# Layer-0 cross attention of a two-layer transformer rewritten in the form of the kernel's self attention

## The chip, the cores and the metric

The kernel runs on one core of one Trainium2 chip. The metric is the device time of one execution in microseconds (us). The core has five engines that run their own instruction streams and wait for each other on semaphores: PE (TensorE, matrix products; its weight loads are listed apart as PEld), DVE (VectorE), ACT (ScalarE), POOL (GpSimd) and SP (SyncE, which here only issues DMAs).

## The reference, cut to what matters

Two layers follow each other over x of shape 2 x 1024 x 256. The change lies in the first block of layer 0, in its second attention, which reads a context of 77 rows:

```
x = layernorm(sa + input_tensor, g1, be1)            # sa: causal self attention, 16 heads of 16
q = einsum('bsd,hde->bhse', x, Wq2)                  # 2 x 16 x 1024 x 16
k = einsum('btd,hde->bhte', encoder_output, Wk2)     # 2 x 16 x 77 x 16
v = einsum('btd,hde->bhte', encoder_output, Wv2) + bv2
p = softmax(einsum('bhse,bhte->bhst', q, k) / 4)
ca = einsum('bhst,bhte->bhse', p, v)                 # heads concatenated
x = layernorm(x + ca, g2, be2)
ffn = relu(x @ Wf1 + bf1) @ Wf2 + bf2
x = layernorm(x + ffn, g3, be3)
```

Everything else of the two layers (self attention before it, the feed-forward nets, layer 1's masked cross attention, its second self attention and its mixture of experts) is as it was.

## The kernel before, in words

The 2048 rows of x are 16 tiles of 128. The program is five written-out instruction streams, one for each engine. PSUM has 8 banks of 512 values; `claim` waits until a bank's last reader is done, `filled` and `arrived` pass a filled bank to its reader, `released` and `drained` tell that the reader is done. Each engine works in the order in which its stream is written.

**Self attention of layer 0** runs in 8 groups of 4 heads. A plan (`attention_plan`) is walked by all engines; its iteration n computes the row maxima of group n (operation "max": PE products, DVE reductions) and, interleaved, the scores, exponentials and value products of group n-1 ("score", "pv"). Operands are packed as bf16 parts in 96 rows; the negated maxima are three more rows (99), so that the exponential is taken straight from PSUM. One step has four scores of up to 512 columns, which pass through two banks (4 and 5) to ACT (L1027), and the value product of the step before (four products of 17 columns each, listed as 128*17), which the plan puts behind the step's third score. A unit of the plan is one score; an iteration has 48 units in 12 steps. Iteration 8 has scores only. Each iteration has one ACT copy of 128x1024 (L1042, "evac") right after its second score, so the starts of these copies mark the iterations. Layernorm "g1" of the four row chunks ("norm", lines 1233 to 1251 and 1350 on DVE) and transposes of the normed rows ("turn") lie in iterations 5 to 7 for chunks 0 and 1.

**Cross attention of layer 0** (`cross(0)`) starts when self attention is done. It runs over 32 units: 16 tiles by 2 halves of 8 heads. A unit is: two float32 products of 128x308 (queries against a block-diagonal key matrix KBD), a maximum over each head's 77 scores on DVE (L1532), the subtraction (L1533), the exponential on ACT (L1074), five transposes of the probabilities (L684), their copies on ACT (L1088), five float32 products with the block-diagonal values (128x136), and for each tile a division and an addition to H on DVE (L1539 to L1544). Query projections, the g1 norms and the turning of chunks 2 and 3, the g2 norms and a small low-rank product lie between the units. Then the first feed-forward product (PE, TRR and WF1P) waits for POOL, which takes the power for the last g2 norm and makes the lower parts of the inputs (L1753). POOL also splits the weights WF1 into two parts behind the second g2 norm (L1726, L1727).

Of the kernel before, what the change touches and what calls it, by code (L numbers as in the profile page):

```python
# [20 lines left out]
P = 128  # L21
# [44 lines left out]


# [21 lines left out]
def attention_plan():  # L89


    for n in range(GROUPS + 1):
# [6 lines left out]
        for u in range(units):  # L99
# [10 lines left out]
            if u == 20 and n in (6, 7):  # L110
                yield "turn", n - 6
            if n == 0:
# [18 lines left out]
    yield "out", GROUPS - 1  # L131


def build(nc, a, out):

    ctx = ExitStack()
    with ctx:
# [31 lines left out]
        def w6(n):  # L169
# [47 lines left out]

        QT = region(0, 4096, "p (g s) -> p g s", g=2)
# [5 lines left out]
        CREP = [[v.rearrange("p (k h t) -> p k h t", k=KC, h=HH) for v in pair]  # L224
                for pair in ((region(27904, 1232), W6[:, 0:1232]), (region(23504, 1232), region(24736, 1232)))]
# [51 lines left out]
        scratch = nc.dram_tensor("qk_parts", [B, 2, D, 3, S], BF16, kind="Internal").ap()  # L277

# [20 lines left out]
        sa_used = sem("sa_used")  # L299
        kv_ready = sem("kv_ready")  # L300
# [87 lines left out]
        def _(pe):  # L388
# [66 lines left out]
            def context(layer, wk):  # L455

                loaded(pe, wk[1])
                loaded(pe, "ctx")
                for g in range(2):
                    claim(("kx", layer, g), [4 + g])  # L460
                    for k in range(KC):
                        ins = mm(PS[:, 4 + g, 0:B * T], wk[0][:, k, P * g:P * g + P], ctxT[:, k, :], start=k == 0, stop=k == KC - 1)
                    filled(ins, ("kx", layer, g))

            def queries(layer, wq, c):

                loaded(pe, wq[1])
                for g in range(2):
                    key = ("q", layer, c, g)
                    claim(key, [4 + g])  # L470
                    for k in range(KC):
                        ins = mm(PS[:, 4 + g, :], wq[0][:, k, P * g:P * g + P],
                                 TR[:, k, 512 * c:512 * c + 512], start=k == 0, stop=k == KC - 1)
                    filled(ins, key)
# [39 lines left out]


# [11 lines left out]
            for op, n, *at in attention_plan():  # L527
# [56 lines left out]
                elif op == "turn":  # L584
# [9 lines left out]
                    filled(ins, ("turn", n))  # L594
                elif op == "out":
                    if n == GROUPS - 1:

                        context(0, (w6(4), "wk2"))
                        queries(0, (w6(3), "wq2"), 0)
# [8 lines left out]
            def low_rank(u):  # L608


# [9 lines left out]
                elif u == 20:  # L620
                    drained(pe, "l2")
                    claim("l3", [bank])
                    for k in range(KC):
                        ins = mm(PS[:, bank, D * k:D * k + D], LD2[:, P * k:P * k + P], UPT)
# [1299 lines left out]
```

## Time and profile before

| | |
|---|---|
| median of 3 runs | 1409.89 us (1409.19 to 1413.25) |
| profiled execution, first to last instruction (span) | 1407.6 us |
| time of the profiled execution itself | not listed apart; its span is 2.3 us under the median of the runs |
| PE busy | 1205.0 us, 86% of the span |
| PE weight loads busy | 882.2 us, 63% |
| DVE busy | 909.1 us, 65% |
| ACT busy | 531.9 us, 38% |
| POOL busy | 313.2 us, 22% |
| mean granted TensorE clock | 0.928 |

A busy share is a mean over stages with different limits. The stage that the change rewrites lies between the last value product of self attention and the first product of the feed-forward net. A matmul's busy time holds its latency, so a high share does not tell that PE works at its peak.

### The profile page before, as it was taken

To read this page: it belongs to the slowest core of one execution; us is meant where nothing else is said; L and a number is where in the kernel's file an instruction comes from. 1 tells how busy PE (TensorE), PEld (TensorE's weight loads), DVE (VectorE), ACT (ScalarE), POOL (GpSimd) and SP (SyncE) were. 2 spreads that over 40 slices of the span, in tenths; PEclk is the share of its full clock that TensorE was granted. 3 is DMA by queue.
4 is the path that set the end of the run, shared out by engine and by line. 5 is a ranking of instruction groups with operands and counts; after the bars stand their busy time and mean duration, and the time that the engine had idled before them with its cause. 6 is when DMAs were issued, how large, how long until landed. Compare 5 with 4: busy or idle time off the path is not lost. (4 is left out here: it accounts for less than half of the span.)

```text
span 1407.6 us, 19711 instructions
## 1 busy us (share of the span) xinstructions
PE 1205.0 (86%) x7056; PEld 882.2 (63%) x7056; DVE 909.1 (65%) x1890; ACT 531.9 (38%) x1149; POOL 313.2 (22%) x491
## 2 busy tenths in 40 slices
PE   5779999797888997978859787799999888899999
PEld 2343333233336775866647666699997667789988
DVE  7487666666516887467766888775653445865555
ACT  1325655555652443524413444201003332543333
POOL 5012222222230021534423655100001011500000
PEclk9798999998988999989987988799999999999999
DMA  4850333330000101000003000000002000000000
GB/s 166 179 136 2 46 47 47 46 47 1 2 1 1 65 1 42 1 0 1 1 1 120 1 1 1 1 0 1 1 18 102 1 0 0 1 1 15 16 16 16
DMA packets 25201, 40.35 MB, mean 29 GB/s; under 512 B 5755, under 2 KB 17041, under 8 KB 24465
## 3 DMA queue, kind: packets, MB, share of 16 engines
q1 hardware_dynamic: 25104, 39.09, 11.7%
q8 instruction: 58, 0.95, 0.3%
q14 instruction: 39, 0.31, 0.1%
HBM read 30.49 MB, written 8.39 MB: 28 GB/s over the span
## 5 line engine op out<-in xcount | busy, mean ns | idle before, releaser
L390 PE MATMUL PS<-ARENA 128*17 128x512 f32 (+14 forms) x2528 | 474.0, 400 | 96.5 <-ACT ARENA L1088 21.2
L390 PEld LDWEIGHTS PS<-ARENA 128*128 128x128 f32 (+4 forms) x2528 | 225.7, 141 | 278.2 <-issue 124.6
L1363 DVE TENSOR_REDUCE ARENA<-PS 128x1 f32<-128x128 f32 (+7 forms) x256 | 180.8, 751 | 77.5 <-PE PS L390 76.4
L1027 ACT ACTIVATE ARENA<-PS 128x512 f32<-128x512 f32 (+3 forms) x384 | 173.6, 490 | 147.1 <-PE PS L390 143.5
L390 PE MATMUL PS<-WQKVP,TRR 128*128 128x384 f32 x512 | 132.1, 339 | 3.1 <-DVE ARENA L1613 2.0
L1773 POOL TENSOR_SCALAR_AFFINE_SELECT ARENA<-ARENA 128x128 f32<-128x128 f32 x256 | 73.6, 292 | 224.6 <-ACT ARENA L1027 221.8
L1745 POOL TENSOR_TENSOR rstd<-var,halves 128x4 f32<-128x4 f32 x36 | 37.9, 1051 | 306.0 <-DVE var L1238 305.8
L390 PEld LDWEIGHTS PS<-W2P,INT 128*128 128x128 f32 x768 | 94.9, 188 | 2.8
L390 PE MATMUL PS<-W2P,INT 128*128 128x256 f32 x768 | 95.6, 280 | 0.0
L390 PEld LDWEIGHTS PS<-WQKVP,TRR 128*128 128x128 f32 x512 | 91.4, 188 | 4.6 <-DVE ARENA L1613 2.6
L390 PE MATMUL PS<-TRR,W1P 128*128 128x512 f32 x256 | 88.6, 408 | 5.8 <-ACT BC L973 5.8
L1615 DVE SCALAR_TENSOR_TENSOR ARENA<-PS,rw,ARENA 128x384 f32<-128x384 f32 x112 | 69.2, 618 | 37.4 <-PE PS L390 36.3
L1673 DVE TENSOR_TENSOR INT<-W,INT 128x512 fp32r<-128x512 f32 x64 | 46.2, 729 | 71.2 <-ACT INT L1196 71.0
L390 PE MATMUL PS<-WQKVP,TRL 128*128 128x384 f32 x256 | 86.1, 336 | 0.0
L390 PE MATMUL PS<-ARENA,TR 128*128 128x256 f32 x320 | 81.3, 412 | 2.8 <-ACT TR L957 1.5
L1074 ACT ACTIVATE ARENA<-ARENA 128x616 f32<-128x616 f32 x64 | 46.0, 718 | 98.7 <-POOL ARENA L1842 64.2
L390 PE MATMUL PS<-TR,W 128*128 128x512 f32 x128 | 68.9, 686 | 8.0 <-DVE ARENA L1270 4.8
L390 PEld LDWEIGHTS PS<-ARENA,TR 128*128 128x128 f32 x320 | 65.5, 210 | 13.5 <-issue 2.6
L1195 ACT ACTIVATE W<-PS 128x512 f32<-128x512 f32 x64 | 38.3, 598 | 93.5 <-issue 82.0
L407 PE MATMUL PS<-ident,H 128*128 128x128 f32 x128 | 30.9, 373 | 41.5 <-DVE H L1228 37.5
L1088 ACT COPY ARENA<-PS 128x512 f32<-128x512 f32 (+1 forms) x128 | 47.7, 424 | 42.5 <-PE PS L684 42.2
L390 PE MATMUL PS<-maskq,identb 128*128 128x128 bf16 x272 | 62.6, 231 | 0.0
(198 smaller groups left out, 1909.4 us busy)
## 6 DMA issues: line engine op xcount, KB each, us to landing
ARENA<-qk_parts SPq DMA_DIRECT2D x96, 128.0 KB, 5.8
qk_parts<-ARENA SPq DMA_DIRECT2D x8, 768.0 KB, 3.3
ARENA<-in_w SPq DMA_DIRECT2D x2, 2048.0 KB, 10.5
ARENA<-in_wqkv SPq DMA_DIRECT2D x1, 3072.0 KB, 10.0
X<-in_x SPq DMA_DIRECT2D x4, 512.0 KB, 8.2
ARENA<-in_wf SPq DMA_DIRECT2D x2, 1024.0 KB, 5.5
out_x<-X SPq DMA_DIRECT2D x8, 256.0 KB, 2.2
BC<-in_bcast SPq DMA_DIRECT2D x1, 1920.0 KB, 12.9
```

What stands on the lines that cost most here:

```text
L390: return nc.tensor.matmul(o, lhsT, rhs, start=start, stop=stop, **kw)
L407: ins = nc.tensor.transpose(PS[:, bank, P * k:P * k + P], src[:, i, P * k:P * k + P], ident[:, :])
L1027: ins = nc.scalar.activation(PROB[GRP * (step % 2) + j][:, 0:w], PS[:, uses[key][0], 0:w], ACT.Exp, scale=HD ** -0.5)
L1074: nc.scalar.activation(EX[u % 4], EX[u % 4], ACT.Exp, scale=HD ** -0.5).then_inc(ex_ready, 1)
L1088: released(nc.scalar.copy(PTS[(u - 1) % 4][0:rows, 4 * m:4 * m + cols, :], PS[0:rows, 4 + m, 0:P * cols].rearrange("p (j s) -> p j s", s=P ...
L1195: nc.scalar.activation(INTF[(2 * n + ic) % 4], src, ACT.Gelu)
L1363: ins = v.tensor_reduce(negm[:, n % 2, TPB * j + st:TPB * j + st + 1], PS[:, bank:bank + 2, :].rearrange("p b s -> p (b s)")[:, 0:P * (st ...
L1615: ins = v.scalar_tensor_tensor(out=QKV[:, i, :], in0=src, scalar=w, in1=QKV[:, i, :], op0=ALU.mult, op1=ALU.add)
L1673: v.tensor_tensor(INT[n % 4][:, 1, ic, :], INTF[(2 * n + ic) % 4], INT[n % 4][:, 0, ic, :].bitcast(F32), ALU.subtract).then_inc(int_ready, 1)
L1745: g.tensor_tensor(rstd[:, 4 * k:4 * k + 4], var[:, 4 * k:4 * k + 4], halves[:, 0:4], ALU.pow).then_inc(rstd_ready, 1)
L1773: g.affine_select(out=prob, in_=prob, compare_op=ALU.is_ge, fill=0.0, base=0, pattern=[[1, P]], channel_multiplier=-1).then_inc(cleared, 1)
```

## The change

Layer 0's cross attention no longer calls `cross`; it becomes operations of the plan.

- **Context, once** ("ctxk", "ctxv", in iteration 1): keys are projected and split into three bf16 parts (ACT, DVE, ACT, DVE), written to memory, and read back as XKEYS, 96 rows for each head, plus three rows of ones (12 DMAs of 16x16x77). Values go to XV with a column of ones.
- **Queries, for each chunk of 512 rows** ("xq", "xqm"): projection in float32 as before, but the result is split into three bf16 parts, written to memory (2 DMAs) and read back into the packed form XPACK (12 DMAs of 16x8x512, like the loads of self attention's packs). Chunk 0 in iteration 7, chunk 1 in iteration 8, chunk 2 ahead of step 4, chunk 3 between the two runs of steps.
- **Maxima** ("xmax", 8 for each chunk): 8 bf16 products of 96 rows and 77 columns, and one DVE reduction over 128x616, negated. Chunks 0 and 1 lie in iteration 8, chunks 2 and 3 in one block between steps 7 and 8. "xneg" transposes the 64 maxima rows, splits them (four short DVE operations) and 6 small DMAs make them rows 96 to 98 of XPACK.
- **Steps** (16: 4 chunks by 4 groups of 4 heads): four scores with the context on the rows (77x512, bf16, 99 rows deep), each with its exponential straight from PSUM; the value product of the step before, behind the third score (four products 17x512); the copy of that product from PSUM to OTS on ACT ("xevac"), at the end of the step; and four transposes of the copy before ("xout"), ahead of the second score, with the division on DVE. No subtraction, no transposes of probabilities, no block-diagonal matrices.
- The g2 norms are operations of the plan ("g2"): chunk 0 and 1 in the block between the runs, 2 at steps 14 and 15, 3 at the end. POOL's split of WF1 follows the power of chunk 1's norm. POOL's clearing of layer 1's value matrix moves behind the first feed-forward inputs.
- The loads of two layer-1 weights (wk3, wv3) move behind the last g2 norm.

```diff
+            if n == 1 and 6 <= u < 16:
+                yield from context_plan(u - 6)
+            if n in (7, 8):
+                c, at = n - 7, u - (8, 2)[n - 7]
+                if at in (0, 2):
+                    yield "xq", c, at // 2
+                if at in (4, 6):
+                    yield "xqm", c, at // 2 - 2
+            if n == GROUPS and u % 2 == 0:
+                if 6 <= u < 22:
+                    yield "xmax", 0, (u - 6) // 2 % 4, (u - 6) // 8
+                if u == 22:
+                    yield "xneg", 0
+                if u >= 32:
+                    yield "xmax", 1, (u - 32) // 2 % 4, (u - 32) // 8
...
+def cross_steps(lo, hi, also):
+    for t in range(lo, hi):
+        yield from also.get(t, ())
+        for j in range(GRP):
+            if j == 1 and t >= lo + 2:
+                yield "xout", t - 2
+            yield "xscore", t, j
+            if j == 2 and t > lo:
+                yield "xpv", t - 1
+        if t > lo:
+            yield "xevac", t - 1
+    yield "xout", hi - 2
+    yield "xpv", hi - 1
+    yield "xevac", hi - 1
+    yield "xout", hi - 1
+
+def cross_plan():
+    yield "norm", 2
+    yield from cross_steps(0, 8, {4: [("turn", 2), ("xq", 2, 0), ("xq", 2, 1), ("xqm", 2, 0), ("xqm", 2, 1)],
+                                  5: [("norm", 3)], 6: [("turn", 3)]})
+    yield "g2", 0, 0
+    yield "xq", 3, 0
+    yield "xq", 3, 1
+    yield "g2", 0, 1
...
+    yield from cross_steps(8, 16, {9: [("rank", 0)], 11: [("rank", 1)], 13: [("rank", 2)], 14: [("g2", 2, 0)], 15: [("g2", 2, 1)]})
+    yield "g2", 3, 0
+    yield "g2", 3, 1
...
+                elif op == "xmax":
+                    i, hh = at
+                    if i == 0:
+
+                        pe.wait_ge(xpack_in[2 * n + hh], 6 * 16)
+                        pe.wait_ge(keys_in, 12 * 16)
+                    first = wide(2)
+                    claim(("xmax", n, i, hh), [first, first + 1])
+                    for h in range(HH):
+                        ins = mm(PS[:, first + h // 4, T * (h % 4):T * (h % 4) + T], XPACK[n][hh][0:ROWS, h, P * i:P * i + P],
+                                 XKEYS[0:ROWS, HH * hh + h, n // 2, 0:T])
+                    filled(ins, ("xmax", n, i, hh))
...
+                elif op == "xout":
+                    drained(pe, ("xv", n))
...
-                    released(v.tensor_tensor(ex, src, most.unsqueeze(3).broadcast_to(full), ALU.subtract), key)
```

In the engines' order of instructions three places matter. In PE's stream the last iteration of self attention had only scores (rows "ARENA 128x...") and value products (17x...):

```order
L390 MATMUL PS<-ARENA 128x512 x4
L390 MATMUL PS<-ARENA 17x512 x4
L390 MATMUL PS<-ARENA 128x512
L390 MATMUL PS<-ARENA 128x384 x3
L390 MATMUL PS<-ARENA 17x512 x4
L390 MATMUL PS<-ARENA 128x384
```

In the changed kernel the same place, a little later in the iteration, holds a maximum of eight 77-column products (rows "W,ARENA") after a step's first and after its third score, the latter ahead of the value product:

```order
L493 MATMUL PS<-ARENA 128x512 x2
L493 MATMUL PS<-W,ARENA 128x77 x8
L493 MATMUL PS<-ARENA 17x512 x4
L493 MATMUL PS<-ARENA 128x512
L493 MATMUL PS<-ARENA 128x384
L493 MATMUL PS<-W,ARENA 128x77 x8
```

What moved: 16 such groups now stand in iteration 8, 8 of them ahead of a value product.

In PE's stream of the cross attention itself one unit of the kernel before reads as follows (scores, value products of the unit before, transposes of the probabilities):

```order
L390 MATMUL PS<-ARENA 128x308 x2
L390 MATMUL PS<-ARENA 128x136 x5
L684 MATMUL PS<-ident,ARENA 128x128 x4
L684 MATMUL PS<-ident,ARENA 104x128
L390 MATMUL PS<-ARENA 128x308 x2
```

and one step of the changed kernel, of which there are 16 in place of the 32 units (scores 77x512, value product 17x512, transposes of the result ident,ARENA):

```order
L493 MATMUL PS<-ARENA,W 77x512 x2
L768 MATMUL PS<-ident,ARENA 128x128 x4
L493 MATMUL PS<-ARENA,W 77x512 x2
L493 MATMUL PS<-ARENA 17x512 x4
L493 MATMUL PS<-ARENA,W 77x512 x2
```

What moved: the transposes now stand between a step's first and second score.

DVE's stream between the two runs of steps has no counterpart before. In the changed kernel it is a norm of chunk 0 (L1666 to L1447), around the split of chunk 3's queries (L1618, L1623), then chunk 2's maxima (L1630) and their parts; behind these rows a norm of chunk 1 and eight more maxima follow:

```order
L1666 TENSOR_TENSOR H<-H,ARENA 128x1024
L1429 BN_STATS stats<-H 128x6 x4
L1432 BN_AGGR mv<-stats 128x2 x4
L1434 TENSOR_SCALAR var<-mv 128x4
L1439 SCALAR_TENSOR_TENSOR H<-H,mv,BC 128x256 x4
L1618 TENSOR_TENSOR ARENA<-PS,ARENA 128x512 x2
L1447 SCALAR_TENSOR_TENSOR H<-H,rstd,BC 128x256 x4
L1623 TENSOR_TENSOR ARENA<-ARENA 128x512 x2
L1630 TENSOR_REDUCE ARENA<-PS 128x8 x8
L1642 CAST ARENA<-PS 64x128
```

What moved: before, these norms lay between units of the cross attention; now the maxima and the next run of steps stand behind them.

## Rows read from the trace of the kernel before

**Rows 1.** Windows: stretch; busy time and instructions of each engine; clock; DMA.

```profile
416.37:563.90 147.53, 127.30 (x728) 98.68 (x728) 114.27 (x251) 56.58 (x123) 22.67 (x22) 0.93 0.08 26
384.07:416.37 32.30, 25.65 (x151) 7.27 (x151) 1.05 (x2) 21.22 (x48) 9.17 (x32) 0.87 0.00 1
```

**Rows 2.** Lines by form, 400 to 640 us: busy us, mean ns; idle before.

```profile
L1533 DVE TENSOR_TENSOR ARENA<-PS,mx 128x616 f32<-128x616 f32 x32 | 25.6, 799 | 1.1
L1532 DVE TENSOR_REDUCE mx<-PS 128x8 f32<-128x616 f32 x32 | 25.4, 794 | 2.4 <-PE PS L390 2.1
L1074 ACT ACTIVATE ARENA<-ARENA 128x616 f32<-128x616 f32 x32 | 23.0, 720 | 34.4 <-DVE ARENA L1533 34.1
```

**Rows 3.** Timeline, one full step of iteration 8: start, us, engine, instruction, idle before.

```profile
406.23 0.10 PEld L390 LDWEIGHTS PS<-ARENA 99*128 99x128 bf16 x1 [0.40 <-ACT ARENA L1027]
...
406.56 1.54 PE L390 MATMUL PS<-ARENA 128*17 128x512 f32 x10
...
407.54 0.11 PEld L390 LDWEIGHTS PS<-ARENA 99*128 99x128 bf16 x2 [0.85 <-ACT ARENA L1027]
407.97 0.60 ACT L1027 ACTIVATE ARENA<-PS 128x512 f32<-128x512 f32 x1 [0.71 <-PE PS L390]
```

**Rows 4.** Timeline, the copy that opens each iteration, and the last one.

```profile
219.90 1.02 ACT L1042 COPY ARENA<-PS 128x1024 f32<-128x1024 f32 x1
256.91 1.02 ACT L1042 COPY ARENA<-PS 128x1024 f32<-128x1024 f32 x1
301.64 1.02 ACT L1042 COPY ARENA<-PS 128x1024 f32<-128x1024 f32 x1
416.42 1.01 ACT L1042 COPY ARENA<-PS 128x1024 f32<-128x1024 f32 x1 [1.19 <-PE PS L390]
```

**Rows 5.** Timeline, query projection, eight transposes, and a bf16 split.

```profile
482.59 3.67 PE L390 MATMUL PS<-TR,W 128*128 128x512 f32 x8
...
422.92 1.04 PE L604 MATMUL PS<-ident,ARENA 128*128 128x128 f32 x8
...
69.40 0.68 DVE L1277 TENSOR_TENSOR ARENA<-ARENA 128x512 bf16<-128x512 f32 x1
```

**Rows 6.** Timeline of DVE, a g1 norm, and one part of negated maxima.

```profile
273.31 1.42 DVE L1350 TENSOR_TENSOR H<-H,ARENA 128x256 f32<-128x256 f32 x4
...
276.70 1.66 DVE L1243 SCALAR_TENSOR_TENSOR H<-H,mv,BC 128x256 f32<-128x256 f32 x4
278.40 1.67 DVE L1251 SCALAR_TENSOR_TENSOR H<-H,rstd,BC 128x256 f32<-128x256 f32 x4
...
377.49 0.28 DVE L1379 TENSOR_TENSOR ARENA<-ARENA 32x128 bf16<-32x128 f32 x1
```

**Rows 7.** Timeline of DVE, a g2 norm beside POOL's split of WF1.

```profile
507.20 4.05 DVE L1243 SCALAR_TENSOR_TENSOR H<-H,mv,BC 128x256 f32<-128x256 f32 x4
```

**Rows 8.** Timeline, the end of the stage.

```profile
559.18 1.18 POOL L1745 TENSOR_TENSOR rstd<-var,halves 128x4 f32<-128x4 f32 x1 [22.86 <-DVE var L1238]
560.33 3.52 POOL L1753 TENSOR_TENSOR TRG<-ARENA,TRR 128x256 fp32r<-128x256 f32 x4
...
563.90 0.79 PE L390 MATMUL PS<-TRR,WF1P 128*128 128x512 f32 x1 [6.11 <-POOL TRG L1753]
```

**Rows 9.** The page's part 6, DMA issues: count, KB each, us to landing; timeline of SP.

```profile
ARENA<-qk_parts SPq DMA_DIRECT2D x96, 128.0 KB, 5.8
qk_parts<-ARENA SPq DMA_DIRECT2D x8, 768.0 KB, 3.3
...
142.73 6.23 SPq L882 DMA_DIRECT2D ARENA<-qk_parts  x12
```

**Rows 10.** Windows of 2 us, columns as in rows 1: a full step, the narrow last steps, the stage's end.

```profile
408.00:410.00 2.00, 1.43 (x11) 0.32 (x10) 0.00 (x0) 1.82 (x4) 0.94 (x4) 1.00 0.00 0
...
414.00:416.00 2.00, 1.18 (x17) 0.29 (x9) 0.00 (x0) 0.28 (x1) 0.64 (x3) 0.50 0.00 0
...
566.00:568.00 2.00, 2.00 (x7) 1.58 (x7) 1.88 (x4) 1.13 (x2) 0.00 (x0) 0.69 0.00 0
```

More of the change, by code:

```diff
@@ L453, in _, with context, queries @@
                 project(0, step)
-            def context(layer, wk):
-                loaded(pe, wk[1])
+            def context(g, bank, wk, name):
+                loaded(pe, name)
                 loaded(pe, "ctx")
[L459 to L474, printed above, removed]
+                key = ("kx", name, g)
+                claim(key, [bank])
+                for k in range(KC):
+                    ins = mm(PS[:, bank, 0:B * T], wk[:, k, P * g:P * g + P], ctxT[:, k, :], start=k == 0, stop=k == KC - 1)
+                filled(ins, key)
+            def queries(c, g, bank, wq, name):
+                loaded(pe, name)
+                key = ("q", name, c, g)
+                claim(key, [bank])
+                for k in range(KC):
+                    ins = mm(PS[:, bank, :], wq[:, k, P * g:P * g + P],
+                             TR[:, k, 512 * c:512 * c + 512], start=k == 0, stop=k == KC - 1)
+                filled(ins, key)
             def gate_input(n, u, first, every):
@@ L732, in _ @@
                     turned("t_xat", s - 2)
-                    queries(1, (w6(5), "wq3"), s - 2)
+                    for g in range(2):
+                        queries(s - 2, g, 4 + g, w6(5), "wq3")
                 if 0 < s < 5:
@@ L753, in _ @@
                 if s == 4:
[L754 removed]
+                    for g in range(2):
+                        context(g, 4 + g, W3[:, 0, :, :], "wk3")
                 if 0 < s < 5:
                     turn("t_xat", "xat", H, s - 1)
[L757 removed]
+            cross()
             for u in range(UNITS, UNITS + 3):
@@ L1777, in self_attention @@
                         power("g1", n)
+                    elif op == "g2" and at[0] == 0:
+                        power("g2", n)
+                        if n == 1:
+                            loaded(pool, "wf1")
+                            for m in range(4):
+                                cols = slice(m * FF // 4, (m + 1) * FF // 4)
+                                split(WF1[:, :, cols], WF1P[0][:, :, cols], WF1P[1][:, :, cols], wf1_split)
                     elif op == "neg" and n == 0:
-                        loaded(pool, "ctx")
                         arrived(pool, ("v1", TILES - 1))
-                        pool.wait_ge(parts_ready, 16)
-                        for b in range(B):
-                            repeat_context(0, b)
+                        g.memset(XKEYS[ROWS:ROWS + 3, :, :, :], 1.0).then_inc(keys_ones, 1)
+                        pool.wait_ge(keys_ones, 1)
                         drained(pool, "simsum")
```

551 lines of the change are left out of this document (360 added, 191 removed).

## The prediction, as it was put on record

> **What bounds the kernel now.** I read the windows by stage first, then the groups of instructions inside the stage, then the timeline of one unit and of one self-attention step. The stage that the change rewrites lasts 147.53 us, from the last value product at 416.37 to the first feed-forward product at 563.90 [rows 1]. In it PE is busy 127.30 us and DVE 114.27: neither is busy throughout, and neither is clear of the other. DVE needs 0.79 us for a unit's maxima and 0.80 for the subtraction, 51 us over 32 units, and ACT, with 0.72 a unit, waits 34.1 us for that subtraction [rows 2]. The loop products, maximum, subtraction, exponential, transposes, copy, products is what sets the pace. In the iteration ahead of it (iteration 8) DVE is busy 1.05 of 32.30 us and POOL 9.17, while ACT is busy 21.22 and PE 25.65 [rows 1]: the place where new maxima would cost DVE nothing.
>
> How a step with context on the rows would run is to be seen in a full step of iteration 8 [rows 3]. The third score's weights load at 406.23, the value product starts at 406.56, the next score's weights load at 407.54, so the eight product rows (two for each float32 product) hold PE for 0.98, and the fourth exponential starts at 407.97, 1.74 after the third score began. ACT had waited 0.71 for it. ACT's exponential of 512 columns takes 0.60 and PE reacts about 0.1 later.
>
> **Part 1, one step.** The new step is that loop plus two things on it: the copy from PSUM (128x512; half of the 1.01 of L1042's 1024 [rows 4], 0.5) sits on ACT between the fourth exponential and the next first one, and the transposes of that copy sit on PE ahead of the second score. Four of them take half of 1.04 [rows 5], 0.5. So from third score to third score: 1.74 to the fourth exponential, 0.6 for it, 0.5 copy, 0.1 reaction, 0.5 transposes, 0.2 for the second score = 3.7 us. Below, if transposes and copy hid wholly, it would be the 2.9 of the step now (1.74, two exponentials of 0.5 to 0.6 back to back, 0.1); above, if nothing of the copy overlapped the exponentials, 4.2. A run of 8 steps has a first step without value product (two pairs of score and exponential, 2.2), a second without transposes (3.2), six full ones (22.2) and a tail: transposes 0.5, value product 1.0, copy 0.6, transposes 0.5, reactions 0.6 = 3.2. Sum 30.8 for 8 steps.
>
> The full step keeps PE's clock only if it is busy enough. In the full steps of iteration 8 PE is busy 1.43 of 2 us and the granted clock is 1.00, the 2.4 GHz level; in the last, narrow steps it is busy 1.18 of 2 and the clock falls to 0.50, the 1.2 GHz level [rows 10]. The new step has about 2.3 us of issued work in 3.7, of which 0.5 is transposes, between the two. By the rows I take it to stay up. The Trainium skill speaks against this: TensorE: Matmul & The Clock Gate, section A second HAM failure mode: psum-queue depth-cycling, says that a kernel which cycles its PSUM banks idles in small pieces often enough to swing between the two clock levels, and section Part 4: PE-mode transpose says that transposes do not count as busy in the same way. By that page the steps would take the longer time that the second rival below works out, and iteration 8 agrees only with the row.
>
> **Part 2, the stage.**
> - Start: copy 1.0, eight transposes 1.0, first scores: 3.0 until the first exponential [rows 4, 5].
> - First run 30.8. Ahead of step 4 lie turn 2 (transposes 1.0, copy 1.0), two query projections 3.67 [rows 5], and the split: ACT, DVE, ACT in turn, about 1.3 behind the projections before the exponentials resume. Against the work that step 3 still covers, 6.5. Turn 3 at step 6 waits for norm 3: DVE starts it at step 4's second score and needs 6.8 (from 273.31 to 280.07) [rows 6], PE comes 1.3 earlier, plus transposes and copy: 2.8.
> - Block between the runs, on DVE, since the next scores stand behind the last maxima's transpose on PE and everything ahead of it on DVE is in order: last division 0.8; norm of chunk 0: addition 1.2 (one of 1024 columns for the four at 1.42), statistics 2.0 (from the additions' end at 274.69 to 276.70), centring 1.7, and 1.7 [rows 6]; four split operations like the 0.68 of L1277 [rows 5], 2.7; 8 maxima of 128x616 at 0.8 [rows 2], 6.6; their parts, four operations near 0.28 [rows 6] with the transpose, 1.6; norm of chunk 1, 6.6 as well, beside POOL's split of WF1, which made the same centring 4.05 instead of 1.66 [rows 6, 7], so 2.5 more; 8 maxima 6.6; transpose and first scores 1.0. Sum 35.0. PE's own pace in the maxima may be worse than DVE's, for it will be at the low clock there: 1.6 more. 36.6.
> - DMA in the block: chunk 3's parts are ready 10 us into it; 3.3 to memory, 12 issues in 6.23 and 5.8 to land [rows 9] = 25. Its maxima are due on DVE at 26. Just hidden.
> - Second run 30.8, plus 1.5 for the low-rank products and 1.5 for starting at the low clock. As the stage start of the feed-forward shows, PE needs a few us of work before the clock is back: 0.69 in the window from 566 [rows 10].
> - End: division 0.8, addition 1.2, statistics 2.0, power 1.2, lower parts 3.5 [rows 6, 8] = 8.7. The norm of chunk 3 now has all of it behind the last transposes, where the present tail is 8.2.
>
> Sum 3.0 + 30.8 + 6.5 + 2.8 + 36.6 + 33.8 + 8.7 = 122.2 against 147.5: 25.3 us less.
>
> **Part 3, what self attention pays.** There the inserted work is hardly hidden. A norm of 6.8 us on DVE made its iteration 44.7 us (256.91 to 301.64) where one without took 37.0 (219.90 to 256.91) [rows 4, 6]: all of it came through.
> - Iteration 1, context: PE eight rows of 154 and eight of 256 columns, 3.0 by the 3.67 for eight of 512; DVE about 2.4. I take 3.0.
> - Iteration 7, chunk 0's queries: PE 3.67, DVE 2.7; 5.0, between 2.7 (they overlap) and 6.4 (they add).
> - Iteration 8: chunk 1's queries at its start, where PE is slow, 5.0. The 16 maxima cost DVE nothing, but PE 0.65 each: between 0.44, when the weight loads pass in pairs as the 0.11 for two at 407.54 [rows 3], and 1.04, the eight float32 transposes [rows 5]. Half stand after a step's first score, where PE has room; half ahead of the value product, on the loop: 8 x 0.65 = 5.2. Sum 10.2, bounds 6 and 16.
>
> Sum 18.2. XKEYS' loads (rows of 154 bytes) and the smaller 1 KB rows of XPACK I cost at nothing: they have most of iteration 3, and more than 10 us in iterations 7 and 8. If that cover is gone, the next iteration waits for its maxima rows, a few us. POOL's clearing, four operations, falls behind the feed-forward's first inputs, where POOL next waits for a norm; likewise nothing, and if it comes late, that norm waits for up to these four operations, some 5 us.
>
> **Forecast.** 18.2 - 25.3 = -7.1 on the span of 1407.6 gives 1400.5. The median of the runs lies 2.3 above that span: 1402.8, say 1402.5.
>
> **The rivals.**
> 1. The added pieces hide and a step keeps its present 2.9: 12 full steps save 0.8 each, 10 us, 2 more if the iteration 8 pieces hide: 1391. For it: ACT waits 0.71 of each step, which could swallow the copy. Against: it waits for PE, which now gets more. 0.17.
> 2. Slower: the clock falls in the steps. At the low level PE's pieces on the loop double: transposes 0.5, second and third score 0.4, value product 1.0, 1.9 us a step. If half of the 12 full steps run so, 1402.5 + 11.5 = 1414; it decides from the third step on (1.9 x 2 = 3.8 takes the time to within the bound of no change, 6 steps beyond it). For it: 0.50 as soon as steps are narrow [rows 10]. Against: 1.00 through all full ones. 0.16.
> 3. The round trips through memory are not hidden (chunk 3's in the block, or XPACK's 1 KB rows take half as long again): 6 us, 1408.5. For it: one microsecond of slack. 0.12.
> 4. The maxima in iteration 8 stop every step, at 1.04 each and none hidden: 16.6 instead of 5.2, with less elsewhere: 1411. 0.07.
>
> **How the numbers follow.** The forecast case has 0.48 and its own range 1397 to 1409. The bounds of the step (2.9 to 4.2) and of the iterations carry the range to 1389 to 1418, which leaves out 2 in 10. A measurement of this kernel tells about 0.3% from no change, so faster is below 1405.7 and slower above 1414.1. Forecast: 0.38 faster, 0.09 same, 0.01 slower. Rival 1: 0.17 faster. Rival 2: 0.07 same, 0.09 slower. Rival 3: 0.09 same, 0.03 slower. Rival 4: 0.03 and 0.04. Together 0.55, 0.28, 0.17.
>
> **What would show it.** In the changed trace: full steps near 3.7 us with the fourth exponential 1.7 behind the third score; a block of 35 us between the runs in which DVE is never idle; iteration 8 near 42 us and iteration 7 near 43; PE's clock near 1.00 in the runs; 120 us between self attention's last value product and the first feed-forward product. Wrong would be: clock 0.50 in the runs, PE waiting for DMA in the block, or DVE idle there.

## The result, and the profile of the changed kernel

The changed kernel takes 1422.93 us (median of 11 runs, 1418.27 to 1425.74), the kernel before 1412.03 (11 runs beside them, 1409.19 to 1419.57). The ratio is 1.0073, 95% interval 1.0057 to 1.0090: 0.7% slower, where 1402.5, so faster, was predicted. The profiled execution has a span of 1420.0 us against 1407.6.

The page's parts 1 to 3 of the changed kernel: busy time, the span in 40 slices of 35.5 us, DMA.

```profile
PE 1194.0 (84%) x6932; PEld 841.4 (59%) x6932; DVE 890.6 (63%) x1862; ACT 532.7 (38%) x1137; POOL 313.2 (22%) x490
...
PEclk9799999899996755989987988899999988999999
...
DMA packets 37967, 50.67 MB, mean 36 GB/s; under 512 B 11098, under 2 KB 28784, under 8 KB 37232
```

By busy time PE (1194.0 us, before 1205.0), DVE (890.6, before 909.1) and POOL (313.2 both times) have no more work than before. The row of the granted clock (PEclk, in tenths of full speed) shows where to look: slices 12 to 15 (426 to 568 us, all of the stage) read 6, 7, 5 and 5, and nothing before them is below 7.

Windows of the changed kernel by piece: start of the stage, first run with what lies in it, block, second run, end, all the rest; then iterations 2 to 4 (answering to 145.55 to 256.91 before), 5 to 7 and 8. Columns as in [rows 1].

```profile
425.46:428.43 2.97, 1.91 (x9) 1.85 (x10) 0.00 (x0) 1.01 (x1) 0.00 (x0) 0.70 0.00 0
428.43:477.70 49.27, 38.02 (x154) 15.29 (x153) 22.29 (x66) 25.61 (x46) 2.34 (x2) 0.74 0.40 85
477.70:511.02 33.32, 14.44 (x138) 9.76 (x138) 31.29 (x62) 2.39 (x4) 10.35 (x10) 0.60 0.46 73
511.02:559.25 48.23, 42.95 (x138) 13.49 (x138) 13.69 (x39) 21.47 (x40) 1.17 (x1) 0.50 0.10 29
559.25:568.21 8.96, 2.09 (x8) 1.03 (x7) 8.62 (x20) 2.40 (x8) 4.66 (x5) 0.50 0.25 74
568.21:1420.00 851.79, 749.06 (x4288) 651.59 (x4288) 535.68 (x1187) 269.38 (x583) 195.33 (x186) 0.92 0.04 13
...
148.96:257.04 108.08, 97.13 (x698) 37.91 (x698) 73.53 (x114) 67.33 (x149) 27.57 (x96) 1.00 0.44 52
257.04:389.81 132.77, 108.09 (x721) 42.90 (x720) 89.29 (x159) 71.53 (x155) 29.98 (x98) 0.92 0.27 40
389.81:425.46 35.65, 31.95 (x287) 13.87 (x286) 17.24 (x26) 22.78 (x53) 8.97 (x31) 0.96 0.45 69
```

The stage lasts 142.75 us (425.46 to 568.21); before, from the same copy of [rows 4], 147.48. It gained 4.7, not 25.3. Self attention ends 9.0 us later (425.46 against 416.42), not 18.2. So the first feed-forward product comes 4.3 us later, and the rest, 851.8 against 843.7 us with the same instructions, adds 8.1. That is the 12.4 of the two spans.

A step at either clock, from the timeline of the changed kernel: start, us, engine, instruction. First one at half clock, then one at full.

```profile
435.15 1.12 PE L768 MATMUL PS<-ident,ARENA 128*128 128x128 f32 x4 [0.73 <-ACT ARENA L1261]
...
436.06 1.06 PE L493 MATMUL PS<-ARENA,W 99*77 99x512 bf16 x2
...
437.05 1.91 PE L493 MATMUL PS<-ARENA 77*17 77x512 f32 x8
...
438.89 1.08 PE L493 MATMUL PS<-ARENA,W 99*77 99x512 bf16 x2
...
440.69 0.69 PE L768 MATMUL PS<-ident,ARENA 128*128 128x128 f32 x2 [0.73 <-ACT ARENA L1261]
...
471.12 0.66 PE L768 MATMUL PS<-ident,ARENA 128*128 128x128 f32 x4 [0.94 <-ACT ARENA L1261]
...
471.61 0.60 PE L493 MATMUL PS<-ARENA,W 99*77 99x512 bf16 x2
...
472.14 1.05 PE L493 MATMUL PS<-ARENA 77*17 77x512 f32 x8
...
474.69 0.55 PE L768 MATMUL PS<-ident,ARENA 128*128 128x128 f32 x3 [1.15 <-ACT ARENA L1261]
```

From transposes to transposes it is 5.54 us (435.15 to 440.69) at clock 0.50, the 1.2 GHz level, and 3.57 us (471.12 to 474.69) at 1.00, the 2.4 GHz level. At half clock PE has no idle time but 0.73 in front of the transposes, 4.8 us of work in 5.54: PE is the bound there, and in the second run (511 to 559 us) it is busy 42.95 of 48.23 us at 0.50 and never comes back.

### The profile page after: what moved, and what is told of

It is laid out like the page before. It is cut to its first block and busy times, and to the rows that moved or that the text cites. A ratio compares the mean times of both kernels' runs of the same rounds, so it can differ in the third digit from the quotient of the medians.

```text
span 1420.0 us, 19533 instructions
## 1 busy us (share of the span) xinstructions
PE 1194.0 (84%) x6932; PEld 841.4 (59%) x6932; DVE 890.6 (63%) x1862; ACT 532.7 (38%) x1137; POOL 313.2 (22%) x490
## 2 busy tenths in 40 slices
DMA packets 37967, 50.67 MB, mean 36 GB/s; under 512 B 11098, under 2 KB 28784, under 8 KB 37232
## 5 line engine op out<-in xcount | busy, mean ns | idle before, releaser
L493 PE MATMUL PS<-ARENA 128*17 128x512 f32 (+14 forms) x2208 | 414.3, 438 | 85.2 <-DVE ARENA L1567 22.7
L493 PEld LDWEIGHTS PS<-ARENA 128*17 128x17 f32 (+5 forms) x2208 | 164.9, 128 | 257.6 <-issue 121.5
L493 PEld LDWEIGHTS PS<-TRR,W1P 128*128 128x128 f32 x256 | 49.4, 193 | 17.5 <-issue 6.8
L1252 ACT ACTIVATE ARENA<-PS 77x512 f32<-77x512 f32 x64 | 36.0, 591 | 61.3 <-PE PS L493 61.0
```

Of the source, the lines that this page charges most:

```text
L493: return nc.tensor.matmul(o, lhsT, rhs, start=start, stop=stop, **kw)
L1252: released(nc.scalar.activation(XPROB[GRP * (n % 2) + j], PS[0:T, uses[key][0], :], ACT.Exp, scale=HD ** -0.5), key)
```

## The experiments

Each ratio is to the kernel before, run on the same chip (its median there: 1413.7, 1412.9, 1417.8 and 1413.2 us in the four sets). "Stage" is counted from the copy that ends self attention to the first feed-forward product in the profiled execution; the expectations of the later sets count it from the last value product, 0.4 us earlier.

**Set 1. Is it the clock, and do the steps hold it?** Filler (products whose results nobody reads) ahead of the second run, in `cross_plan`; PE's part:

```
     yield "g2", 1, 1
+    yield "fill", 0, 3
...
+    yield "fill", 1, 4
     yield "xneg", 3
+                elif op == "fill":
+                    first = wide(1)
+                    claim(("fill", n), [first], readers=0, signals=0)
+                    for _ in range(at[0]):
+                        mm(PS[:, first, :], w6(3)[:, 0, 0:P], TR[:, 0, 0:512])
```

> The changed kernel with filler ahead of the second run of steps: TensorE makes 3 products of 128x128 by 512 (f32, results unread) in the idle 5.74 us before the maxima of chunk 3, and 4 more right before the shifts of chunk 3. In the changed kernel the second run (511 to 559 us) stands at clock 0.50 throughout, with a full step of 5.54 us; steps 4 to 7, after the projections of chunk 2, stood at 1.00 with 3.57 us. Theory A (the steps keep the level they start at; dense work ahead raises it): clock 1.00 in steps 8 to 15, step 3.57 us, second run about 8 x 1.97 = 15.8 us shorter, filler costs 3.4 us at full clock to 6.7 us at half, so the first FFN product comes 9 to 12 us earlier and the median is near 1412. Theory B (the steps themselves pull the clock down wherever they start): the clock falls again within two or three steps, the gain is under 6 us and the filler's cost eats it: 1420 to 1427. Theory C (the step is set by the order of transposes and copies, the clock aside): step stays over 5 us even at 1.00.

Measured: ratio 0.9966 (0.9932 to 1.0000), median 1408.9, runs from 1395 to 1414; stage 131.8 us. Windows of this kernel, one in the first run and the second run:

```profile
458.00:478.00 20.00, 17.15 (x63) 6.10 (x63) 5.30 (x15) 8.74 (x16) 0.67 (x1) 0.50 0.83 148
514.00:548.00 34.00, 26.36 (x143) 9.38 (x141) 14.27 (x41) 21.38 (x40) 1.17 (x1) 1.00 0.11 34
```

The second run stood at 1.00 for all of its 34 us with a step of 3.57, as theory A said; theory C is out. From its first score to its last transposes that run takes 31.1 us (516.21 to 547.26), and 48.2 in the changed kernel (511.02 to 559.25) with the same instructions. But steps 5 to 7 of the first run, which held 1.00 in the changed kernel, were at 0.50 here: a step's own products hold the clock sometimes. The wide spread of the runs fits that; only one of them was profiled.

Filler ahead of step 0 as well (`yield "fill", 2, 4` in front of `yield "xneg", 1`).

> As the one with filler before step 8, and 4 more such products between the output transposes of the last group and the shifts of chunk 1, so ahead of step 0, where the changed kernel ran steps 0 to 3 at 0.50 and 5.54 us. Theory A: clock 1.00 in all 16 steps, 3 full steps of the first run shorter by 1.97 us and the projections of chunk 2 by some 3 us, so 9 us gained for 3.4 to 6.7 us of filler: 2 to 6 us below the kernel with filler before step 8 alone. Theory B: the steps fall back to 0.50, and it is 3 to 7 us above it.

Measured: 1.0031 (1.0009 to 1.0052), stage 135.7. The clock was 1.00 from 431 to 434 us, a mean of 0.54 from 434 to 449, and 1.00 again in the second run. The first run did as theory B says, the second as theory A: filler in front alone is not enough.

Chunk 2's and 3's queries, maxima and the norms among 16 steps instead of in a block; the packs' loads go ahead of the feed-forward weights on SP's queue.

```
+    yield from cross_steps(0, 16, {3: query(2) + [("norm", 3)], 6: query(3), 7: [("g2", 0, 0), ("g2", 0, 1)],
+                                   8: rows(2), 10: [("g2", 1, 0), ("g2", 1, 1)], 11: rows(3),
+                                   12: [("rank", 0)], 13: [("rank", 1)], 14: [("rank", 2), ("g2", 2, 0)], 15: [("g2", 2, 1)]})
```

> One run of 16 steps without the block between them: queries of chunk 2 at step 3 and of chunk 3 at step 6, maxima of chunk 2 before step 8 and of chunk 3 before step 11, norms of the cross attention at steps 7, 10 and 14; loads of the chunks' packs ahead of the FFN weights. VectorE has some 87 us of work in the stage (two norms of 6.5, four of 8.5, 16 divisions of 0.68, 16 maxima of 0.77 and shifts of 2.4 each for 4 chunks), TensorE 65 us at full clock. If the block's VectorE work and its waits for TensorE and DMA were what kept the stage at 142.8 us: the two overlap, the wait before step 8 is for the pack and rows of chunk 2 (some 10 us at most), and the stage comes to 90 to 105 us at clock 1.00, so the median to 1372 to 1387. If the steps run at 0.50 all the way, TensorE is the bound with 16 x 5.54 and 13 us for turns, projections and maxima: 100 to 115 us, median 1383 to 1397. If the packs' DMA bounds it (1 KB rows, 16 us for a chunk), step 8 starts after 480 us and the median is 1395 or more.

Measured: 1.0025 (1.0003 to 1.0047), stage 137.6. None of the three numbers: it was the half-clock case, and I had added up PE too low. Windows of this kernel:

```profile
430.00:482.00 52.00, 42.32 (x143) 16.87 (x145) 27.92 (x80) 26.00 (x47) 3.51 (x3) 0.66 0.36 71
498.00:556.00 58.00, 51.30 (x218) 19.71 (x218) 29.91 (x69) 22.19 (x41) 10.38 (x10) 0.50 0.18 53
```

PE is busy 51.3 of 58 us at 0.50, DVE half of the time. With the clock down, it hardly matters where DVE's work stands: 5 us of the block's 33 came out of it.

The maxima of chunk 1 and their shifts moved from iteration 8 to the place ahead of step 2.

> The 8 maxima units of chunk 1 and its shifts moved from iteration 8 of self attention to the place before step 2. Iteration 8 lasts 35.65 us in the changed kernel and 32.03 before the change. If a unit costs its products' 0.45 us in full there, iteration 8 becomes 32 us; if half of them lie in waits for ScalarE's exponentials, 33.8; if they cost 0.65 us each (as the prediction had it), 30.4. In the stage the units cost VectorE's 0.77 us each (6.2 us) plus 2 us for the shifts and less than nothing if the clock comes up. So the median is 1422 to 1429.

Measured: 1.0119 (1.0086 to 1.0153), stage 149.2. Iteration 8 became 34.70 us (388.75 to 423.45) from 35.65, and 35.21 in a second trace of the changed kernel (run r13_after, below). The median, 1427.2, is in the range, but the iteration is none of the three. In the other eleven variants, which leave iteration 8 alone, it lasts 35.2 to 35.7 us, so a unit of chunk 1's maxima costs it 0.06 to 0.13 us, not 0.65. Chunk 0's eight units, earlier in the iteration, were not moved.

**Set 2. What holds it?** Products in each step, where PE waits for ACT's copy. A full product here has weights of 128 rows by 128 columns, a thin one 77 by 17, as the step's value products have:

```
                 elif op == "xout":
-                    drained(pe, ("xv", n))
                     first = wide(1)
                     claim(("xo", n), [first])
+                    for _ in range(4):
+                        mm(PS[:, first, :], w6(3)[:, 0, 0:P], TR[:, 0, 0:512])
+                    drained(pe, ("xv", n))
```

> The changed kernel with 4 more products in every step, in the place where TensorE waits for ScalarE's copy ahead of the output transposes (0.94 us idle at full clock, 0.73 at half): 128x128 by 512, f32, on data already in SBUF, into the bank that the transposes then overwrite. Four cost 0.86 us at full clock (3.60 us for 8 chunk-query products), 1.7 to 2.9 at half. If denser work of full products brings the clock up and holds it: steps at 1.00, 3.6 to 3.9 us each, and the 12 full steps that stood at 0.50 gain 1.7 us each, about 20 us with the projections of chunk 2: median near 1403. If the clock doesn't answer to it, each step at 0.50 grows from 5.54 to 6.5 or more, 12 us in all: 1435.

Measured: 1.0166 (1.0127 to 1.0205), stage 157.3. The clock came up and held; the price was mine. Four f32 products by 512 take 3.60 us at full clock (the record counts them as 8, as in [rows 5]), so a step became 5.85 us.

Next, the same with `mm(PS[0:VW, first, :], w6(3)[0:T, 0, 0:VW], TR[0:T, 0, 0:512])`, 77 rows by 17 columns.

> As the one with 4 full products in every step, but of the value products' shape: 77 rows and 17 columns by 512, in the same place, the same time on TensorE (0.13 to 0.22 us each at full clock). If the time that TensorE is busy is what counts, the clock comes up and holds as with full products: near 1403. If products of this shape do nothing for the clock, steps stay at 0.50 and grow by 0.3 to 1 us: 1426 to 1437.

Measured: 1.0554 (1.0511 to 1.0598), stage 201.8. Windows of the kernel with four full products a step, then of the one with four thin ones:

```profile
519.00:529.00 10.00, 8.49 (x36) 2.44 (x34) 3.45 (x8) 3.82 (x7) 0.00 (x0) 0.50 0.02 5
534.00:574.00 40.00, 40.00 (x163) 16.87 (x162) 12.21 (x34) 16.00 (x30) 1.17 (x1) 1.00 0.13 36
```

```profile
434.00:484.00 50.00, 48.81 (x194) 14.65 (x193) 15.58 (x43) 20.07 (x36) 1.17 (x1) 1.00 0.43 83
524.00:614.00 90.00, 90.00 (x186) 19.77 (x179) 12.22 (x34) 17.70 (x33) 1.17 (x1) 0.50 0.06 16
```

Both second runs begin at 0.50. With full products PE is at 1.00 from 534 us on. With thin ones it is busy 90 of 90 us and stays at 0.50, while the first run, which entered at 1.00, stays there for 50 us. In both traces of the changed kernel the first run enters at 1.00 too, and is at 0.50 by 434 us. So PE's busy time alone does not bring the clock back, though without gaps the level that was there was kept. The profiled execution of the thin kernel is one of two at 1474.7 us; the other four took 1490 to 1493, so the 50 us at 1.00 may be the rarer course. Nor is a thin product cheap; the timeline of the thin kernel at full clock, four of them, 0.90 us each:

```profile
438.32 3.61 PE L493 MATMUL PS<-TR,W 77*17 77x512 f32 x8
```

The order of set 1's third kernel with four full products a step, and set 1's first kernel with two:

> The version with one run of 16 steps (chunk 2's and 3's maxima and the norms among the steps), plus 4 full products in every step. Without them it stood at clock 0.50 in all but some six steps, with full steps of 5.54 us and a stage of 137 us (428 to 565). If full products hold the clock: steps of 3.6 to 3.9 us, TensorE 13 us of other work, the wait for chunk 2's pack and rows before step 8 grows by what the steps gain (6 us now, 10 to 18 then), and the stage comes to 105 to 115 us: median 1388 to 1398. If they don't: 1428.

> The kernel with filler ahead of step 8 (its second run stood at 1.00 throughout in the profile, its times spread from 1395 to 1414), plus 2 full products in every step. If the steps need some full products to hold a clock that is up: the second run is at 1.00 in all executions, the first too from step 5, and the median comes from 1408.9 to near 1400. If a step with its own products holds the clock once it is up and the spread is from elsewhere: no better than 1409, since the first run pays 2 x 0.43 us in each step at half clock.

Measured: 1.0100 (1.0069 to 1.0132), stage 147.1; and 0.9986 (0.9960 to 1.0013), stage 131.3. The clock was at 1.00 in most steps of either, which took 5.85 and 4.12 us: it was kept, and paid for in full. Both medians that were hoped for (1388 to 1398, and near 1400) were missed for that price.

**Set 3. The same, cheaper.** One product of 384 columns a step, 0.68 us, less than the wait of 0.94:

```
-                    for _ in range(4):
-                        mm(PS[:, first, :], w6(3)[:, 0, 0:P], TR[:, 0, 0:512])
+                    mm(PS[:, first, 0:384], w6(3)[:, 0, 0:P], TR[:, 0, 0:384])
```

> The kernel with filler ahead of step 8, plus one full product (128x128 by 384, f32) in every step, in the 0.94 us wait ahead of the output transposes. The runs before showed what I had wrong: an f32 product by 512 costs 0.90 us at full clock (3.60 for 4, which the profile counts as 8 records), so 4 in a step cost 3.6 us and 2 cost 1.88; this one costs 0.68 and fits into the wait. With 4 or 2 full products in a step the clock was at 1.00 in both runs (steps of 5.85 and 4.12 us). If 0.68 us a step holds it too: steps of 3.6 to 3.7 us in both runs, the stage 131.8 minus 16 x 0.45 = 124 to 126 us, median 1402 to 1406. If it takes more of them: the first run falls to 0.50 again after the projections of chunk 2 as with filler before step 8 alone, and the median is 1407 to 1412.

> The same with the step's extra product in the value products' shape (77 rows, 17 columns, by 384): the same time on TensorE. With 4 thin products a step TensorE was busy without a gap and the clock kept the level it had: 1.00 from 430 to 489 us, 0.50 from 519 to past 594 us. If thin work neither raises nor (without gaps) lowers the clock: the second run, which starts at 1.00 after the filler, stays there as in the kernel without them, the first run starts at 0.50 and stays there until the projections of chunk 2; steps at half clock cost 0.6 us more. Median 1408 to 1416, 4 to 10 us above the one with the full product. If busy time is what counts, it equals the one with the full product within 3 us.

Measured: 0.9885 (0.9865 to 0.9905), 1401.9 us, stage 124.9; and with the thin product 0.9926 (0.9910 to 0.9942), 1407.0, stage 131.6. Both came as expected, but for 1 us. Windows of the kernel with the full product, first and second run:

```profile
431.00:480.00 49.00, 40.69 (x190) 18.35 (x188) 27.37 (x82) 26.67 (x48) 3.51 (x3) 0.90 0.41 85
514.00:546.00 32.00, 28.65 (x153) 11.50 (x154) 13.99 (x41) 21.03 (x40) 1.17 (x1) 1.00 0.15 41
```

And of the one with the thin product, first run before and after the projections of chunk 2:

```profile
434.00:444.00 10.00, 10.00 (x34) 2.81 (x32) 3.39 (x10) 4.29 (x9) 0.12 (x1) 0.50 0.01 2
454.00:479.00 25.00, 21.13 (x108) 7.69 (x108) 14.57 (x41) 14.33 (x26) 1.17 (x1) 1.00 0.76 164
```

With the thin product PE is busy 10 of 10 us at 0.50, and only the projections, full products, end that. The two kernels differ in nothing but the shape of that one product, and their intervals do not overlap. With the full product the first run is not at 1.00 throughout either (0.90 in the mean); it falls to 0.50 and is back by 442 us, ahead of the projections, where the thin kernel comes back at 452, behind their start. In the second run both are at 1.00.

The order of set 1's third kernel with this product, chunk 2's maxima at step 7, and full products in two waits:

> The version with one run of 16 steps, now with chunk 2's maxima at step 7, a full product by 384 in each step, 2 full products by 512 before step 0 and 6 in the wait for chunk 2's rows before step 8. With 4 full products a step this order stood at 1.00 and took 147.6 us for steps of 5.85 us; without any, 138.0 us at 0.50. If 0.68 us a step holds the clock: steps of 3.65 us, so 16 x 2.2 = 35 us less than 147.6, and the wait before step 8 grows by some 10 us as pack and rows of chunk 2 come no sooner: 115 to 125 us for the stage, median 1391 to 1402. If the clock falls: 135 to 140 us, 1414 to 1420.

Measured: 0.9797 (0.9782 to 0.9813), 1388.4 us, stage 113.7, a little better than the best that was expected. The move of DVE's work was worth 5 us at half clock (142.75 to 137.6); with the clock held the stage is 11 shorter (124.9 to 113.7). That is not the move alone: this kernel also has chunk 2's maxima a step earlier and its filler in other places.

**Set 4. The part behind the stage, and what is left of the stage.**

> The kernel before, unaltered, for a second trace of the part behind the stage. From the first FFN product to the end its first trace has 843.7 us; the changed kernel has 851.8 with the same instructions, and the nine variants 846.6 to 856.7. If the part's time changes from execution to execution with the granted clock: this trace has 846 to 852 at a clock lower than the first's. If the change moved something in the part: 843 to 845 again.

> The changed kernel, unaltered, for a second trace. The part behind the first FFN product: 846 to 856 us if it varies by execution, 851 to 852 again if it doesn't. The stage: 143 us within 3, with steps 8 to 15 at clock 0.50 as in the first trace if the steps cannot raise the clock by themselves; the first run's steps at either level, since there the projections of chunk 2 raise it and nothing but chance holds it.

Measured: the kernel before has 852.5 us behind its first feed-forward product (559.73 to 1412.2) where its first trace had 843.7; the changed kernel 849.7 (569.35 to 1419.0) where it had 851.8. The stage is 143.0 and 145.0. Windows of the second trace of the changed kernel: right behind the projections, later steps of the first run, second run.

```profile
449.00:455.00 6.00, 4.33 (x21) 1.48 (x19) 4.34 (x10) 3.89 (x8) 0.00 (x0) 1.00 0.27 107
457.00:479.00 22.00, 19.15 (x69) 7.17 (x68) 6.38 (x20) 9.05 (x16) 1.17 (x1) 0.50 0.78 140
511.00:560.00 49.00, 42.74 (x137) 13.30 (x138) 14.51 (x41) 21.48 (x40) 1.17 (x1) 0.50 0.09 28
```

The second run is at 0.50 again; the first run lost the clock two steps after the projections, where the first trace had it in all of these steps but for a dip at turn 3. And the last 850 us of the kernel before differ by 8.8 us between two executions.

The last version puts the maxima one or two at a time between scores, and frees the end of the stage:

```
+    for j in range(GRP):
+        also.setdefault((7, j), []).extend(units[2][2 * j:2 * j + 2])
+        also.setdefault((9, j), []).extend(units[3][j:j + 1])
+        also.setdefault((10, j), []).extend(units[3][GRP + j:GRP + j + 1])
...
+                        if n == 3:
+                            lower_parts(0)
                         power("g2", n)
...
-            pe.wait_ge(wf1_split, 4)
             turn("t_g2", "g2", H, 0)
+            pe.wait_ge(wf1_split, 4)
```

> The version with one run of 16 steps and a full product in each, with four more moves: the 8 maxima units of chunk 2 stand between the scores of step 7 and those of chunk 3 between the scores of steps 9 and 10 (before: in blocks ahead of steps 8 and 11, where TensorE waited for VectorE's 0.78 us a unit, 7 us each time); 4 instead of 6 full products in the wait ahead of step 8; GpSimd splits the first FFN weights behind the norm of chunk 1 and not of chunk 2, and makes the lower parts of chunk 0 ahead of the last norm's power; TensorE waits for the weights' split behind the first FFN transposes (2.67 us and 5.39 us of waits at the stage's end). The stage was 114.2 us. Expected if these waits are what is left: 7 us at chunk 3, 2 to 4 us at chunk 2, 5 us at the end, so 98 to 102 us and a ratio to the kernel before of 0.969 to 0.974 against 0.980. If VectorE's queue takes the place (its divisions come behind the norms, and the banks with them): 108 us or more, 0.976 to 0.98.

Measured: 0.9816 (0.9783 to 0.9849), 1385.7 us, stage 108.2: 5.5 us less than the version before it in the stage, and no difference in the ratio that the two intervals tell. The 98 to 102 us that were expected are missed; by the stage it is the second branch. The two longest waits of PE in this kernel's stage, and a window behind the first of them:

```profile
PE PS L487 <- DMA ARENA<-ARENA: 6.2, 2, 3.6
PE PS L487 <- ACT ARENA L1252: 2.9, 5, 1.0
```

```profile
484.00:489.00 5.00, 5.00 (x30) 1.89 (x28) 1.46 (x3) 2.37 (x5) 0.00 (x0) 0.50 0.82 283
```

But these rows do not show VectorE's queue as the cause. The largest wait is for the transfers that carry a chunk's maxima rows (6.2 us, ahead of steps 8 and 12), and behind the first of them PE is at 0.50 again for some steps. What either is worth was not tried.

## Why the prediction was wrong

**The step that failed** is the sentence "By the rows I take it to stay up". The size of a step was right: it takes 3.57 us at clock 1.00, predicted 3.7 (its terms add to 3.64) with bounds 2.9 to 4.2, and loses 1.97 at 0.50, as the second rival had it with 1.9. But the rival's case was given 0.16, and it came in larger than drawn: all of the second run and part of the first stood at 0.50, where the sum has all steps at 1.00. By pieces, with the predicted ones in brackets:

- Start 2.97 (3.0).
- First run with turn 2, projections and turn 3 49.3 (40.1): two of the full steps ahead of step 4 at 5.54, and projections that took 6.70 and not 3.67.
- Block 33.3 (36.6). DVE is busy 31.29 of it. It is as DVE-bound as said. PE waited 4.1 us for chunk 3's pack, which the prediction named as a sign of being wrong, but that wait cost nothing. The pack was there 20.5 us into the block (498.22), where 25 was said, while DVE was in chunk 1's norm until 504.33, 26.6 us into it, where 26 was said. The transfer was hidden, by 6 us, and the third rival did not happen here:

```profile
498.22 1.22 PE L493 MATMUL PS<-W,ARENA 96*128 96x77 bf16 x16 [4.08 <-DMA ARENA<-xq_parts]
...
500.15 4.26 DVE L1447 SCALAR_TENSOR_TENSOR H<-H,rstd,BC 128x256 f32<-128x256 f32 x4
504.33 3.09 DVE L1630 TENSOR_REDUCE ARENA<-PS 128x8 f32<-128x616 f32 x4
```

- Second run 48.2 (33.8).
- End 8.96 (8.7).

The sum is 142.75 against 122.2: 9.2 + 14.4 for the two runs, less 3.3 for the block. That it is the clock, and not the pieces, is shown by the second run with filler ahead of it, 31.1 us at 1.00 against 48.2 at 0.50 with the same instructions, and by the kernel with one full product a step: its stage is 124.9 us.

Why did the rows mislead? I judged the new step by PE's busy share, 2.3 of 3.7 us between two rows at either level [rows 10]. The rows between those two already spoke against it:

```profile
410.00:412.00 2.00, 1.53 (x13) 0.44 (x12) 0.00 (x0) 1.27 (x4) 0.85 (x4) 1.00 0.00 0
412.00:414.00 2.00, 1.53 (x16) 0.49 (x12) 0.00 (x0) 1.15 (x5) 1.25 (x5) 0.91 0.01 4
```

The clock fell in the second of them, with PE busy 1.53 of 2 us in both, more than the 1.43 that I took as the mark of a step that holds it; the 1.18 was read where the clock was down already. The runs say the same: 90 of 90 us busy with thin products at 0.50, 26.4 of 34 us busy at 1.00. What they show to matter is the shape of what is added: in the same place, in steps at 0.50, full products brought the clock to 1.00 and thin ones did not. The full step of iteration 8 that I compared with has score products of 99x128; the new ones are 99x77, and its value products 77x17. What a product is shaped like was in no term of my sum. That the narrower shapes are why the step loses a clock of 1.00 is not shown: no run changes the shape of the step's own products, and the same steps kept 1.00 in some places and lost it in others.

The Trainium skill's warning, TensorE: Matmul & The Clock Gate, section A second HAM failure mode: psum-queue depth-cycling, agrees in the outcome (a clock that swings between the levels in such a loop: 1.00 and 0.50 in one run of steps). It names small idle gaps as the cause. The steps in which the clock fell have waits of 0.2 us and more, but so has the run that stayed at 1.00 for 34 us; and gaps do not explain the low level, since the 90 us had none. The transposes, the other doubt that the prediction raised, do not keep the clock down here. In the first trace of the changed kernel it fell to 0.50 in a wait and was back at 1.00 before 468 us, behind little else than transposes, twelve of 128x128:

```profile
464.67 1.97 PE L711 MATMUL PS<-ident,H 128*128 128x128 f32 x8 [2.24 <-DVE H L1447]
466.43 0.64 PE L493 MATMUL PS<-ARENA,W 99*77 99x512 bf16 x1
466.86 0.97 PE L768 MATMUL PS<-ident,ARENA 128*128 128x128 f32 x4
```

**Self attention** was priced too high, 18.2 against 9.0: the inserted work cost some 12.3, and 3.3 came back elsewhere. Iteration 1 paid 3.4 (3.0) and iteration 7 4.8 (5.0; 6.8 in the second pair of traces). Iteration 8 paid 3.6 (1.7 in the second pair of traces), where 10.2 was said and 6 was the lower bound: the term "8 x 0.65 = 5.2" was wrong, since a unit costs about 0.1, which leaves, if all 16 are alike, 2 us or less for the projections, where 5.0 was said. Part of that may be the clock, which is 0.87 and 0.82 over the iteration before the change and 0.96 and 0.97 with it; no run holds it fixed. And iterations 2 to 4 took 108.08 us at clock 1.00 where they had taken 111.36 at 0.96; in the second pair of traces it was 108.0 against 110.8. No edit touches their products; why the clock no longer dips there was not tried. In the variants that leave self attention as it is, its end lies at 423.2 to 429.0 us, so the 9.0 is one value of some 7 to 13. The fourth rival (maxima at 1.04 each) was the opposite of what happened; the first (pieces hide) held for the copy no better, since at 1.00 a step is 3.57, not 2.9.

**The rest of the span.** I had it unchanged. In one pair of traces it was 8.1 us longer, in the second pair 2.8 shorter. Over both pairs self attention ends 8.3 us later (9.0 and 7.6), the stage is 1.4 us shorter (143.9 against 145.2), and the rest is 2.6 longer, with 8.8 between executions of one kernel. The sum, 9.6, is the 10.9 of the medians within what the rest varies; whether the 2.6 belong to the change stays open. So in these two pairs the change buys 1 us in the stage and pays 8 in self attention. The stage of the kernel before varied too, 147.5 and 143.0, and neither swing was in my bounds.

**What held**: the costs at DMA level (XKEYS and 1 KB rows at nothing: there are some 12,800 more packets, 37967 against 25201, and between 108 and 424 us neither PE nor DVE waits for a DMA), the block, the end, the size of a step. With the clock held (one full product a step) the kernel is 1.15% faster than the kernel before beside it, 15.9 us by the medians, where 7.1 was forecast for the change as made. Its trace has less: 22.6 us gained in the stage against 147.48, and 12.6 paid in self attention (428.98 against 416.42), so the first feed-forward product comes 10.1 us earlier. The rest of the 15.9 has no trace of the kernel before beside it and stays open.

## What to carry to other kernels

When a change replaces matmuls by narrower ones, price its loop at both clock levels before choosing, and ask whether PE is the bound at the lower one (here 4.8 us of PE work where the step at full clock lasts 3.6). If so, do not count on a high busy share to bring the clock back: in both traces of this kernel the second run began at 0.50 and stayed there for all of its 48 us. A full-size product placed in a wait that exists anyway cost 0.68 us of idle time a step and was worth 0.8% here (0.9885 against 0.9966), and only then was moving VectorE's work among the steps worth having: 0.980 with both (and filler in two waits), 1.0025 with the move alone.

## What was unexpected of the hardware

- PE busy without a gap for 90 us, at clock 0.50 from beginning to end (products of 77 rows and 17 columns, 99x77, and transposes); with full 128x128 products in the place of the added thin ones it rose and stayed at 1.00.
- The same thin products kept a clock of 1.00 for 50 us. So what went before bears on the level of such a loop, but it does not settle it: behind the same projections the unaltered steps kept 1.00 in one execution of the changed kernel and lost it after two steps in another.
- An f32 product of 77x17 by 512 takes as long as one of 128x128 by 512: 0.90 us at full clock alone, while four of the step's value products side by side in different columns of the array take 1.05 together.
- The same instructions behind the stage took 843.7 us in one execution of the kernel before and 852.5 in another.
